# A fused two-layer Flamingo kernel on one core: VectorE's row maxima and subtractions of the attention taken in pairs, with the residual, the logits and the choice of experts between the two pairs

## What is computed

```python
x = x + tanh(g_xattn[0]) * L0_xattn(layernorm(x), ctx, ctx, ...)   # 16 heads of 8, 64 tokens per batch
x = x + tanh(g_ffn[0])   * L0_ffn(layernorm(x), Wg, W1, W2, W3)    # 8 experts, the best 2 per token
x = x + tanh(g_xattn[1]) * L1_xattn(layernorm(x), ctx, ...)
x = x + tanh(g_ffn[1])   * L1_ffn(layernorm(x), ...)               # 8 experts, the best 2 per token
# L0_xattn: scores = q k' / sqrt(8); probs = softmax(scores); out = (probs v) wo' + wo_b
# L0_ffn:   logits = x @ Wg; top 2; w = softmax(top 2); out = sum of w * (silu(x W1) * (x W2)) W3
```

## Time and profile before

| what | value |
|---|---|
| three timed executions | 534.97, 537.22, 538.54 us (median 537.22) |
| span of the profiled execution, first to last instruction | 534.4 us |
| TensorE busy, share of the span | 487.3 us, 91% |
| VectorE busy | 420.5 us, 79% |
| ScalarE busy | 316.8 us, 59% |
| GpSimd busy | 234.2 us, 44% |
| stage A, until `a_nrm` of the last unit | until 224 us |

### The profile page before, as it was taken

The page is one execution under the profiler, slowest core; times in us unless marked ns, Lnnn a source line. Parts: engine busy times, 40 slices in busy tenths (PEclk is TensorE's granted clock), DMA queues, the critical chain, the costliest instruction groups (busy, mean ns, idle before and its releaser), DMA issues. The chain is left out here.

```text
span 534.4 us, 14733 instructions
## 1 busy us (share of the span) xinstructions
PE 487.3 (91%) x4456; PEld 394.8 (74%) x4456; DVE 420.5 (79%) x1690; ACT 316.8 (59%) x777; POOL 234.2 (44%) x328
## 2 busy tenths in 40 slices
PE   2688999998999989989999999998998999989997
PEld 1366777776767767777888888775887888779897
DVE  4788899999999969777766667685779995777973
ACT  1567877677776667545566665557553557454553
POOL 3322255545555465543330366541458864224420
PEclk9999999899999999999999999999999999999999
DMA  9603011000100121125675344331000112000011
GB/s 245 277 11 91 21 36 32 29 29 29 34 29 29 38 72 41 36 68 158 178 207 165 104 131 118 89 95 36 21 27 20 45 47 69 12 0 1 2 41 39
DMA packets 48129, 36.85 MB, mean 69 GB/s; under 512 B 6466, under 2 KB 43970, under 8 KB 47812
## 3 DMA queue, kind: packets, MB, share of 16 engines
q1 hardware_dynamic: 31332, 21.13, 13.3%
q0 software_dynamic: 4640, 9.45, 6.2%
q10 hardware_dynamic: 12096, 5.51, 3.7%
HBM read 22.44 MB, written 13.63 MB: 67 GB/s over the span
## 5 line engine op out<-in xcount | busy, mean ns | idle before, releaser
L474 POOL DMA_INDIRECT yg<-done,gidx x64 | 64.4, 1007 | 40.2 <-PE bank L1604 17.8
L1638 PE MATMUL bank<-QK 128*64 128x256 f32 x512 | 70.8, 399 | 11.1 <-DVE Pr L909 5.7
L458 POOL DMA_INDIRECT sent<-xr,rowu x60 | 58.9, 981 | 43.2 <-DVE rowu L1014 22.0
L440 POOL TENSOR_TENSOR ve<-mv,half 128x4 f32<-128x4 f32 (+1 forms) x40 | 8.9, 222 | 122.5 <-DVE mv L826 121.5
L1205 DVE TENSOR_TENSOR act<-sil,bank 128x256 f32<-128x256 f32 x80 | 33.6, 420 | 33.5 <-ACT sil L667 33.2
L617 ACT ACTIVATE PT<-bank 128x512 f32<-128x512 f32 x64 | 36.4, 602 | 35.7 <-PE bank L1604 34.9
L1638 PEld LDWEIGHTS bank<-QK 128*64 128x64 f32 x512 | 32.5, 139 | 29.8 <-DVE Pr L909 8.7
L667 ACT ACTIVATE sil<-bank 128x256 f32<-128x256 f32 x80 | 30.8, 384 | 39.4 <-PE bank L1794 39.4
L1810 PE MATMUL bank<-f0w_s,aT 128*128 x320 | 50.0, 279 | 0.7 <-DVE yb L1211 0.6
L905 DVE TENSOR_REDUCE mx<-bank 128x8 f32<-128x512 f32 x64 | 43.7, 682 | 4.2 <-PE bank L1638 4.0
L909 DVE TENSOR_TENSOR Pr<-bank,mx 128x512 f32<-128x512 f32 x64 | 43.7, 683 | 1.2
(11 more groups left out here) (237 smaller groups left out, 1323.0 us busy)
## 6 DMA issues: line engine op xcount, KB each, us to landing
xb<-sent SPq DMA_DIRECT2D x80, 64.0 KB
done<-yb ACTq DMA_DIRECT2D x80, 64.0 KB
cT<-ctx_t_dram SPq DMA_DIRECT2D x16, 128.0 KB, 2.1
f0w_s<-f_w_dram SPq DMA_DIRECT2D x1, 2048.0 KB, 11.1
Pr<-ctx_t_dram SPq DMA_DIRECT2D x8, 256.0 KB
QK<-ctx_tok_dram SPq DMA_DIRECT2D x8, 256.0 KB
out_dram<-xs SPq DMA_DIRECT2D x8, 256.0 KB, 2.3
xs<-x_dram SPq DMA_DIRECT2D x2, 512.0 KB, 5.7
```

Source lines behind the costliest of these rows:

```text
L458: nc.gpsimd.indirect_dma_start(sent, bass.IndirectOffsetOnAxis(ap=rowu[:, s, 2 * k + c:2 * k + c + 1], axis=0), rows[:, c, :], None).then_ ...
L474: nc.gpsimd.indirect_dma_start(yg[:, s, j, :], None, done[u // (U4 // HALVES)], bass.IndirectOffsetOnAxis(ap=gidx[:, s, j:j + 1], axis=0)) ...
L1638: last = mm(bank[g % 2][L * b:L * (b + 1), 256 * p:256 * (p + 1)], QT[:, s, g, t:t + L], Kb[:, s, :, t:t + L], start=True, stop=True)
```

## The change

`it_a` of VectorE is rewritten. In each turn the maxima of groups 0 and 1 come first, then their two subtractions; then follow the first weight, the residual of unit u-1, the logits, the second weight, the statistics, the largest logits, the experts and the moments; then the maxima of groups 2 and 3 and their two subtractions. The number of instructions and their shapes are the same, the semaphores and the values waited for are the same, and the lists of TensorE, ScalarE, GpSimd and SyncE are not touched.

```diff
                 if has(u + 1):
                     a_max(u + 1, 0)
+                    a_max(u + 1, 1)
                 if isinstance(u, int) and u == UT:
                     t_blocks()
                 if has(u + 1):
                     a_sub(u + 1, 1 - s, 0)
+                    a_sub(u + 1, 1 - s, 1)
                 if isinstance(u, int) and u == UT:
                     t_ends()
-                if has(u + 1):
-                    a_max(u + 1, 1)
+                if has(u - 3):
+                    first_weight(1, u - 3, 2, 2, 1.0, kept_weight(u - 3, 0))
+                if has(u - 1):
+                    a_x(u - 1)
                 if isinstance(u, int) and u == UT:
                     t_owner(0)
-                if has(u + 1):
-                    a_sub(u + 1, 1 - s, 1)
+                if has(u - 2):
+                    logits(1, u - 2, 2, bank[3][:, 2 * P:2 * P + 2 * E].rearrange("p (c e) -> p c e", e=E))
+                if has(u - 3):
+                    second_weight(1, u - 3, 2, kept_weight(u - 3, 0), kept_weight(u - 3, 1))
+                if has(u - 1):
+                    sums(1, u - 1, 2)
...
+                if has(u - 2):
+                    largest(1, u - 2, 2)
+                    experts(1, u - 2, 2)
+                if has(u - 1):
+                    moments(1, u - 1, 2)
                 if has(u + 1):
                     a_max(u + 1, 2)
...
+                    a_max(u + 1, 3)
...
                 if has(u + 1):
                     a_sub(u + 1, 1 - s, 2)
+                    a_sub(u + 1, 1 - s, 3)
```

More of the change, by code:

```diff
@@ L1146, in it_a @@
                     a_sub(u + 1, 1 - s, 0)
+                    a_sub(u + 1, 1 - s, 1)
                 if isinstance(u, int) and u == UT:
                     t_ends()
-                if has(u + 1):
-                    a_max(u + 1, 1)
+                if has(u - 3):
+                    first_weight(1, u - 3, 2, 2, 1.0, kept_weight(u - 3, 0))
+                if has(u - 1):
+                    a_x(u - 1)
                 if isinstance(u, int) and u == UT:
                     t_owner(0)
-                if has(u + 1):
-                    a_sub(u + 1, 1 - s, 1)
+                if has(u - 2):
[4 more added lines that the diff above has]
+                    sums(1, u - 1, 2)
                 if isinstance(u, int) and u == UT:
                     t_expert(0)
-                if has(u - 3):
-                    first_weight(1, u - 3, 2, 2, 1.0, kept_weight(u - 3, 0))
+                if has(u - 2):
[3 more added lines that the diff above has]
+                    moments(1, u - 1, 2)
                 if has(u + 1):
                     a_max(u + 1, 2)
-                if has(u - 3):
-                    second_weight(1, u - 3, 2, kept_weight(u - 3, 0), kept_weight(u - 3, 1))
+                    a_max(u + 1, 3)
                 if isinstance(u, int) and u == UT:
```

## The result

The new order takes 559.10 us (median of four executions, 557.89 to 562.85) against 536.41 us for the kernel before (four, 534.97 to 538.54). The ratio is 1.0437, with a 95% interval of 1.0401 to 1.0472: slower by 22.7 us. The profiled execution has a span of 557.0 us, 22.6 more than the earlier trace rows.

A forecast was written before the change was run, and what follows sets the result against it. VectorE's full list was taken to set the turn, TensorE having little room. Loop 7.5 and outside 10.4 (17.9) plus clock falls 4.5 gave 22.4 us on the 537.2 median: 559.6 us; 8-in-10 range 549 to 567.

The forecast's parts named there:

- The ring: Stage A loop: waits through VectorE and TensorE make each turn 13.89 us, 0.94 more; chance 0.78 with few clock falls.
- The loop: Stage A's eight loop turns: each 0.94 us longer than 12.95, together 7.5 us slower.
- Where the time outside the loop comes from: Stage A turns outside the loop: later group 2 scores and a longer tail behind the residual, 10.4 us slower.
- The start: Turn 0 and the one before: no residual, they pay for later subtractions 0, 2 and 3, 1.5 us together.
- The clock: TensorE in stage A: three falls to 1.2 GHz at 1.6 us each, less 0.3, 4.5 us slower.
- VectorE stays the bound and the holding is gone: Rival, loop: projection ready, weights no longer held by GpSimd's subtraction, 7.6 us less, 529.6 us; chance 0.04.
- Only TensorE's delay counts: Rival, stage A: VectorE's longer tail is covered, each of 16 turns pays 0.6 us, 9.6 in all, 547 us; chance 0.06.
- The clock falls in most turns: Rival, TensorE before `a_v`: ten falls instead of three add 11 us, 571 us; chance 0.09.

The follow-up runs named there:

- the last run above: Changed kernel plus early projection and logits on TensorE, GpSimd's weight subtraction between its stores, ScalarE's exponentials of groups 0 and 1 before its last copy: 534.50 us, ratio 0.9972.
- The run with one move too many: Changed kernel plus early projection, GpSimd's moved subtraction, group 3 scores ahead of TensorE's last transposes, ScalarE's two exponentials ahead of its last copy: 539.35 us, ratio 1.0071.
- the old order (527.9 us): Kernel before plus early projection and logits on TensorE, GpSimd's subtraction between its stores, ScalarE's two exponentials ahead of its last copy: 527.86 us, ratio 0.9858.

## Why the prediction was right

559.6 us was predicted and 559.1 measured, and the mechanism named is the one that the rows show. By the steps:

- *The ring.* Walked from an `a_v` at 0: scores of group 1 end at 3.55 predicted, 3.55 measured (87.34 + 1.08 - 84.87); sub 0 at 4.22, 4.21; scores of group 2 at 4.97, 4.94; projection's end at 8.11, 8.08; residual at 8.28, 8.25; `att` at 13.41, 13.37; the turn 13.89, 13.85. Each distance came from a row of the old trace. That worked because an in-order list keeps its distances as long as it waits in the same places; all that had to be found was the new waits.
- *The loop*, 7.5 us: 9.5 less one fall of 1.6 is 7.9. The 0.4 over is that some turns take 14.15 instead of 13.85. VectorE is idle for 0.20 us there ahead of the positions, where the row names no engine but "issue", and reaches its first maximum later. The walk of the one turn didn't contain it.
- *Where the time outside the loop comes from*, 10.4 us: turns 1, 2, 11 and 14 came to 6.8 against 7.3. Turns 12 and 13 came to 2.7, of which a fall is 1.6; 1.1 remain against 1.6.
- *The start* was mis-sized: "1.5 together" for turn 0 and the one before it, measured 4.1. The later subtractions were there, as forecast. But the step took the durations of the old trace, where the score matmuls were fast from 22.3 us on, and in the new one they were so only from about 28.6. The profiled executions with the first pair in turn 0 fall in two kinds. With the pair alone, with the early projection, and with that and GpSimd's move, the matmuls were fast by 23 us but the granted clock fell to 0.50 once more near 35, and `att` of turn 0 came at 41.0 to 41.8. In the kernel after, with the second pair undone, and in the last run above, they were fast late and no fall followed, and `att` came at 42.7 to 42.9. The run with one move too many had some of both, fast by 26.6 us and a fall at 37, and 43.67. In the six executions without the first pair there it came at 37.8 to 39.2, with no fall. So the pair there costs some 2 us or more either way. What decides between the kinds stays open.
- *The clock* was mis-sized the other way: three falls, 4.5 us, were taken, and two came up to the last `att` of this execution, 3.2 us. The 4.5 holds a slip of 0.3: the fall of the old turn 6 was taken off, though the mean of 12.95 us, which the loop's 7.5 was counted from, already contained it. The price of a fall was right: 15.47 against 13.85 is 1.6. The two errors (+2.6 at the start, -1.3 here, the rest small) cancel to 0.7 at the last `att`, so the half microsecond between forecast and median is partly luck. The number of falls is not fixed either: the mean granted clock was 0.991 in this execution and 0.982 to 0.988 in the other three.
- *VectorE stays the bound and the holding is gone*: the holding was real, though worth less than the 7.6 us given there (the move of GpSimd's subtraction alone wins 4.7 us), and the new order does end it. It was refused on one number, the projection's end at 8.11, and that number decided: once the projection stood earlier, the loop fell from 113.06 to 101.20. The holding also came back once in the new trace. In the turn with the fall VectorE came late to the first weight, at 161.73, beside GpSimd's subtraction from 161.28 to 162.56, and was held until 162.60; in the other seven turns it took 0.22 to 0.26 us. The Trainium skill, in SBUF — State Buffer, section Who interferes with whom, has an exclusive lock on the port pair that VectorE and GpSimd share, and names `tensor_scalar` among the operations that can take it; the trace agrees in that the operation that came second ended with the first, but in which mode this `tensor_scalar` ran no run here shows. The prediction read the second weight of turn 4 as in agreement with the rule that the first to start holds the port. That fits the end of the hold, 84.30; by the rows the weight started first, at 82.85 against GpSimd's 83.00, and was the one held.
- *Only TensorE's delay counts* (0.6 us a turn, 547): refuted. Without the first pair's delay 14.1 of the 22.7 us are still there.
- *The clock falls in most turns*: refuted, though the idle time at the end of a turn grew from 0.44 us to 0.84 + 0.45.

## What to carry to other kernels

On an engine that works through its list in order, an instruction that waits for another engine is dear by what stands behind it. Before such an instruction is moved ahead, find its producer's end in the other engine's list and subtract. If the new place comes earlier than that, move the producer first; here four lines on TensorE were worth 20 us.

A pair of independent operations of this size (128 x 512 numbers) saves a tenth of a microsecond per dependent step on VectorE, and delays the first result by a whole operation, 0.61 us. Here it paid where nobody waited for that first result (the second pair, 0.27 us a turn) and cost 0.64 us a turn where TensorE did.

When a wait hides another cost, as the wait for the projection hid the held weights, removing the wait brings the other cost back, so both have to be treated; and the treatment may be worth more on the old order (527.9 us) than on the new one (534.5).

## What was not expected of the hardware

- A 128 x 2 operation of VectorE is held before GpSimd's row begins. With the early projection the second weight started at 86.56 and would have been over by 86.72, but GpSimd's subtraction has its row from 86.84. The hold ended with it, at 88.15 against 86.84 + 1.28 = 88.12. The same is seen in the kernel before: in turn 5 the first weight starts at 94.99 and is held until 96.96, GpSimd's row is from 95.65 to 96.93. In turn 4 a first weight that started 0.88 us ahead of that row took 0.22 us. GpSimd's fourth indirect store has its row just ahead of the subtraction in all three, so whether it is the subtraction or the store that holds first stays open, and the times of GpSimd's rows are rough.
- TensorE's clock fell to the 1.2 GHz level behind short idle times, 0.83 and 0.44 us with small matmuls and transposes between them, in turn 9, and not in turns 4 and 5 with the same idle times. A fall lasts about 3 us (once 7) and costs 1.6 us of a turn on the ring.
- At the start of the program eight score matmuls take 1.98 us at first and 1.08 later. The change came by 25 us in some executions and at 28.6 in others. The kernel after is of the late kind and the one with the early projection of the early kind, though their lists are the same up to there, so it need not be the kernel that decides. What does stays open, since each was profiled once.
